# The values product of a 16-head attention with V as the stationary operand in 32-column strips

## The reference

```python
logits = einsum("bhqd,bhkd->bhqk", q, k) / sqrt(16)     # + mask * -1e9, or -inf where masked
attn = softmax(logits, axis=-1)
out = einsum("bhqk,bhkd->bhqd", attn, v)                # back to (b, q, 256), then @ wo + bo
```

## Time and profile before

| | |
|---|---|
| median of 3 runs | 2276.11 us (2273.66 to 2279.21) |
| profiled execution: span from the first to the last instruction | 2271.6 us |
| PE / PEld busy | 1858.7 us (82%) / 1510.4 us (66%) |
| DVE / ACT / POOL busy | 1292.4 us (57%) / 1100.7 us (48%) / 1022.0 us (45%) |
| the chain that ended last | PE 53%, DVE 12%, ACT 7%, issue 5% |
| mean granted clock of TensorE | 0.908 of full speed |

### The profile page before, as it was taken

How to read it: one execution, slowest core, us unless ns; L and a number is a source line. 1 busy time by engine, 2 the same in 40 slices (tenths; PEclk the granted TensorE clock), 3 DMA queues, 4 the chain that set the end, 5 groups by cost and what they waited for, 6 DMA issues and landing times.

```text
span 2271.6 us, 32211 instructions
## 1 busy us (share of the span) xinstructions
PE 1858.7 (82%) x10033; PEld 1510.4 (66%) x10049; DVE 1292.4 (57%) x2343; ACT 1100.7 (48%) x3186; POOL 1022.0 (45%) x911
## 2 busy tenths in 40 slices
PE   4666667566875776776999899999988999999997
PEld 3565556454664664665777777777766787787776
DVE  6877778557558557558445455454533635436361
ACT  1111221446546556556646465564644665556562
POOL 4566665545446436446333354433533423333330
PEclk8889998777887888888999999999989999999999
DMA  7100000000200000000000200000000000000000
GB/s 216 69 5 5 9 5 5 5 1 5 79 1 5 5 1 5 5 0 5 6 1 6 79 0 9 0 5 5 1 5 5 6 6 0 5 23 0 9 1 10
DMA packets 31293, 34.87 MB, mean 15 GB/s; under 512 B 3196, under 2 KB 30040, under 8 KB 30808
## 3 DMA queue, kind: packets, MB, share of 16 engines
q1 hardware_dynamic: 31192, 33.70, 4.7%
HBM read 31.60 MB, written 2.10 MB: 15 GB/s over the span
## 4 chain that ended last, share of the span: by engine, by line
PE 53%; DVE 12%; ACT 7%; issue 5%; POOL 1%; DVEq 0%; ACTq 0%; POOLq 0%
PE ps L496 28%; PE ps L653 9%; PE ps L675 8%; PE ps L663 5%; ACT work L797 4%; DVE xn L843 3%; PE ps L507 3%; DVE shifts L978 1%; ACT hT L718 1%; DVE work L996 1%; ACT work L788 1%; DVE QKb L818 1%; DVE QT L816 1%; DVE work L972 1%; DVE shifts L981 1%
## 5 line engine op out<-in xcount | busy, mean ns | idle before, releaser
L496 PE MATMUL ps<-hT,w_slot 128*128 128x256 f32 x1856 | 449.9, 396 | 27.6 <-ACT hT L718 20.8
L496 PEld LDWEIGHTS ps<-hT,w_slot 128*128 128x128 f32 x1856 | 356.6, 197 | 78.2 <-ACT hT L718 23.7
L1145 POOL TENSOR_TENSOR work<-KT,own_head 128x512 f32<-128x512 f32 x256 | 261.3, 1047 | 289.4 <-ACT KT L730 236.1
L663 PEld LDWEIGHTS ps<-ident,work 128*128 128x128 f32 x1536 | 212.7, 154 | 140.8 <-issue 100.0
L653 PE MATMUL ps<-work,QT 128*128 128x512 f32 x512 | 274.2, 617 | 22.8 <-POOL work L1145 20.6
L855 DVE TENSOR_TENSOR x_all<-ps,x_all 128x512 f32 (+1 forms) x88 | 60.8, 691 | 380.4 <-PE ps L496 331.3
L800 ACT ACTIVATE work<-work,shifts 128x128 f32<-128x128 f32 x768 | 244.8, 392 | 66.4 <-DVE shifts L976 64.8
L663 PE MATMUL ps<-ident,work 128*128 128x128 f32 x1536 | 259.9, 297 | 16.9 <-DVE work L996 16.9
L788 ACT ACTIVATE work<-ps 128x512 f32<-128x512 f32 (+1 forms) x384 | 229.2, 597 | 82.0 <-PE ps L675 54.9
L797 ACT ACTIVATE work<-ps,shifts,score_scale 128x128 f32<-128x128 f32 x512 | 228.3, 471 | 67.7 <-DVE shifts L981 67.7
L675 PEld LDWEIGHTS ps<-V,work 128*128 128x128 f32 x2048 | 251.2, 192 | 7.4 <-issue 4.4
(11 more groups left out here) (114 smaller groups left out, 3040.3 us busy)
## 6 DMA issues: line engine op xcount, KB each, us to landing
ctx_in<-in_ctx SPq DMA_DIRECT2D x32, 256.0 KB, 2.7
w_slot<-in_L_xattn_W SPq DMA_DIRECT2D x2, 1024.0 KB, 6.3
w_slot<-in_L_xattn_ff_w SPq DMA_DIRECT2D x1, 2048.0 KB, 11.3
w_slot<-in_L_xattn_ffn_w SPq DMA_DIRECT2D x2, 1024.0 KB, 8.5
w_slot<-in_L_xattn_w SPq DMA_DIRECT2D x2, 1024.0 KB, 9.8
out<-x_all SPq DMA_DIRECT2D x8, 256.0 KB, 2.1
x_all<-in_x SPq DMA_DIRECT2D x1, 1536.0 KB, 11.6
pad<-in_mask_Bx1x1xS_fk SPq DMA_DIRECT2D x1, 1024.0 KB, 7.2
```

Source lines behind the costliest of these rows:

```text
L496: mm = pe.matmul(dst, lhsT(k), rhs(k), start=(k == 0), stop=(k == chunks - 1))
L663: mm = pe.transpose(bank(2 + u % 2)[:, tok(h)], prob[u % NP][:, tok(h)], ident[:, :])
L1145: pool.tensor_tensor((KBb if quant else KB)[u % NK].rearrange("p (h k) -> p h k", h=HU), keys, own[:, half * HU:(half + 1) * HU].unsqueeze ...
```

## The change

V becomes the stationary operand and the transposed probabilities stream. The output partitions that a strip writes must start at a multiple of 32 and a head is 16 wide, so two heads share a strip: `Vz` holds for each pair four blocks of 16 columns, `[V of head 0, zeros, zeros, V of head 1]`. The product of head `e` takes blocks `2e` and `2e+1` (32 columns), and the two heads of a pair accumulate into the same 32 output partitions. A unit of 4 heads is still 4 products, alternating between two strips. The output has its 256 features on the partitions, so in layers 1 to 3 `outputs` writes `OT`, and the transposes of `O` and their copy go.

The column of ones goes too. In layers 2 and 3 VectorE reduces the exponentials (`row_sums`, two units late), and per sequence takes the reciprocals and spreads them over 16 columns a head (`inverses`). TensorE turns these with two transposes (`inverse_rows`), ScalarE copies them out (`inv_T`), and VectorE multiplies (`outputs`, a step later than before). `O` of the two streams serves as the buffers for the inverses. The vector columns are loaded into `gate`, the quantised V lies in `Vz`'s space, and only four query biases are kept scaled. `Vz` is zeroed once by GpSimd and once more by VectorE before layer 2.

```diff
-        V = two("V", [P, G, H, DH + 1])
+        Vz = two("Vz", [P, G, H // 2, 4, DH])
...
+        Vzb = [b.rearrange("p g a x d -> p (g a x d)")[:, 0:G * D].bitcast(BF16).rearrange("p (g a x d) -> p g a x d", g=G, x=4, d=DH) for b in Vz]
...
+        oinv = rowinv
+        inv_cols = O[0].rearrange("p g (h d) -> p g h d", h=H)
+        inv_T = O[1].rearrange("p g (c t) -> p g c t", c=C)
...
+                sp.dma_start(gate[c0:c0 + n, 0, 0:P], src_of(name).rearrange("(c p) -> c p", p=P)).then_inc(s["vrows_loaded"], 16)
...
+        SUMS_AT = 2
...
-                        pe.wait_ge(s["o_ready"], G * (phase("mix", layer, g, n["mix"] - 1, st) + 1))
-                        turned(one, O[st]).then_inc(q["ot_ps"], 1)
+                        if layer == 0:
+                            pe.wait_ge(s["o_ready"], G * (phase("mix", layer, g, n["mix"] - 1, st) + 1))
+                            turned(one, O[st]).then_inc(q["ot_ps"], 1)
                     elif piece == "y":
-                        pe.wait_ge(q["ot_ready"], use("out", layer, g, n["out"]) + 1)
+                        if layer == 0:
+                            pe.wait_ge(q["ot_ready"], use("out", layer, g, n["out"]) + 1)
+                        else:
+                            pe.wait_ge(s["o_ready"], G * (phase("mix", layer, g, n["mix"] - 1, st) + 1))
                         for j in range(G):
                             mm = product(other[:, j * D:(j + 1) * D], lambda k: OT[st][:, k, tok(j)], lambda k: w[arg["w"]][:, k, :], C)
                         mm.then_inc(q["y_ps"], 1)
...
                 def values(u):
-                    j = u // UJ
+                    j, m = u // UJ, u % UJ // 2
                     pe.wait_ge(s["PT_ready"], U * ap + u + 1)
                     if u % UJ == 0:
                         pe.wait_ge(s["o_ready"], G * (mp - 1) + j + 1)
-                    for h in range(HU):
-                        hh = u % UJ * HU + h
-                        rhs = Vb[st][:, j, hh * DH:(hh + 1) * DH] if quant else V[st][:, j, hh, :]
-                        mm = pe.matmul(bank(4 + j)[:, hh * width:(hh + 1) * width], (PTb if quant else PT)[u % 2][:, tok(h)], rhs,
-                                       start=True, stop=True)
+                    for e in range(2):
+                        for x in range(2):
+                            pair = u % UJ * 2 + x
+                            at = pair % 4 * 32
+                            lhsT = (Vzb if quant else Vz)[st][:, j, pair, 2 * e:2 * e + 2, :]
+                            mm = pe.matmul(bank(4 + j)[at:at + 32, m * S:(m + 1) * S], lhsT, (PTb if quant else PT)[u % 2][:, tok(2 * x + e)],
+                                           start=(e == 0), stop=(e == 1))
                     mm.then_inc(s["o_ps"], 1)
+                def inverse_rows(j):
+                    pe.wait_ge(s["inv_cols_ready"], G * np_ + j + 1)
+                    for m in range(C):
+                        mm = pe.transpose(bank(4 + j)[:, D + m * S:D + (m + 1) * S], inv_cols[:, j, m * HC:(m + 1) * HC, :], ident[:, :])
+                    mm.then_inc(s["inv_ps"], 1)
                 def step(i):
                     if i < U:
                         scores(i)
                     if 0 <= i - lag < U:
                         turn(i - lag)
-                    if 0 <= i - lag - 1 < U:
-                        values(i - lag - 1)
+                    u = i - lag - 1
+                    if 0 <= u < U:
+                        values(u)
+                        if not quant and u % UJ == UJ - 1:
+                            inverse_rows(u // UJ)
...
-                    elif piece == "ot":
+                    elif piece == "ot" and layer == 0:
...
+                    u = i - lag - 1
+                    if not quant and 0 <= u < U and u % UJ == UJ - 1:
+                        j = u // UJ
+                        act.wait_ge(s["inv_ps"], G * np_ + j + 1)
+                        act.activation(inv_T[:, j, :, :].rearrange("p c t -> p (c t)"), bank(4 + j)[:, D:2 * D], ACT.Copy)\
+                            .then_inc(s["inv_T_ready"], 1)
...
-                            quantise(Vb[st].rearrange("p g d -> p (g d)"), O[st].rearrange("p g d -> p (g d)"), other, d, at, q["v_ready"], G)
+                            quantise(Vzb[st].rearrange("p g a x d -> p (g a) x d")[:, :, 0:4:3, :],
+                                     O[st].rearrange("p g d -> p (g d)"), other, d, at, q["v_ready"], G)
...
+                            if j == 0 and layer == 2 and n["att"] == 0 and isinstance(g, int) and g == 0:
+                                dve.memset(Vz[st][:, :, :, :, :], 0.0).then_inc(s["V_zeroed"], 1)
+                                dve.wait_ge(s["V_zeroed"], st + 1)
+                            dve.tensor_tensor(Vz[st][:, j, :, 0:4:3, :], other[:, j * D:(j + 1) * D].rearrange("p (a x d) -> p a x d", x=2, d=DH),
+                                              row(arg["b"] % "v").rearrange("p (a x d) -> p a x d", x=2, d=DH), ALU.add).then_inc(q["v_ready"], 1)
...
+                def row_sums(u):
+                    dve.wait_ge(s["exp_ready"], U * ap + u + 1)
+                    dve.tensor_reduce(rowsums[:, u * HU:(u + 1) * HU], prob[u % NP].rearrange("p (h k) -> p h k", h=HU), AX.X, ALU.add)\
+                        .then_inc(s["sums_ready"], 1)
+                def inverses(j):
+                    dve.wait_ge(s["sums_ready"], U * np_ + UJ * (j + 1))
+                    dve.reciprocal(oinv[:, j, :], rowsums[:, j * H:(j + 1) * H]).then_inc(s["oinv_ready"], 1)
+                    dve.wait_ge(s["oinv_ready"], G * np_ + j + 1)
+                    dve.wait_ge(s["inv_ps"], G * (np_ - 1) + j + 1)
+                    inv = oinv[:, j, :].unsqueeze(2).broadcast_to([P, H, DH])
+                    if masked and arg["mask"] == "drop":
+                        dve.tensor_scalar(inv_cols[:, j, :, :], inv, live[:, 2:3], None, ALU.mult).then_inc(s["inv_cols_ready"], 1)
+                    else:
+                        dve.tensor_copy(inv_cols[:, j, :, :], inv).then_inc(s["inv_cols_ready"], 1)
                 def outputs(j):
                     dve.wait_ge(s["o_ps"], U * ap + UJ * (j + 1))
+                    o = bank(4 + j)[:, 0:D].rearrange("p (c t) -> p c t", c=C)
                     if quant:
-                        dve.tensor_scalar(O[st][:, j, :], bank(4 + j)[:, 0:D], out_scale[:, arg["quant"]:arg["quant"] + 1], None, ALU.mult)\
+                        dve.tensor_scalar(OT[st][:, :, tok(j)], o, out_scale[:, arg["quant"]:arg["quant"] + 1], None, ALU.mult)\
                             .then_inc(s["o_ready"], 1)
                         return
-                    o = bank(4 + j)[:, 0:H * (DH + 1)].rearrange("p (h d) -> p h d", h=H)
-                    nth = G * use("att_phase", layer, g, ST * mix + st) + (j + 1 - G * BEFORE["att_phase"][2])
-                    dve.reciprocal(oinv[:, j, :].unsqueeze(2), o[:, :, DH:DH + 1]).then_inc(s["oinv_ready"], 1)
-                    dve.wait_ge(s["oinv_ready"], nth)
-                    inv = oinv[:, j, :].unsqueeze(2).broadcast_to([P, H, DH])
-                    if masked and arg["mask"] == "drop":
-                        dve.scalar_tensor_tensor(out=O[st][:, j, :].rearrange("p (h d) -> p h d", h=H), in0=o[:, :, 0:DH],
-                                                 scalar=live[:, 2:3], in1=inv, op0=ALU.mult, op1=ALU.mult).then_inc(s["o_ready"], 1)
-                    else:
-                        dve.tensor_tensor(O[st][:, j, :].rearrange("p (h d) -> p h d", h=H), o[:, :, 0:DH], inv, ALU.mult)\
-                            .then_inc(s["o_ready"], 1)
+                    dve.wait_ge(s["inv_T_ready"], G * np_ + j + 1)
+                    dve.tensor_tensor(OT[st][:, :, tok(j)], o, inv_T[:, j, :, :], ALU.mult).then_inc(s["o_ready"], 1)
...
+                    u = i - SUMS_AT
+                    if not quant and 0 <= u < U:
+                        row_sums(u)
+                        if u % UJ == UJ - 1:
+                            inverses(u // UJ)
+                    u = i - lag - (1 if quant else 2)
...
+            for n, name in enumerate(Q_BIASES):
+                at = col_at[name][0]
+                q_bias = dve.tensor_scalar(vcols_q[:, n * C:(n + 1) * C], bank(0)[:, at:at + C], float(DH) ** -0.5, None, ALU.mult)
+            q_bias.then_inc(s["tables_ready"], 1)
...
-                pool.memset(V[st][:, :, :, :], 1.0).then_inc(s["consts_ready"], 1)
+                pool.memset(Vz[st][:, :, :, :, :], 0.0).then_inc(s["consts_ready"], 1)
...
```

More of the change, by code:

```diff
@@ L102 @@
 PER_PASS["local_phase"] = [ST * n for n in PER_PASS["local"]]
+PER_PASS["natt_phase"] = [ST * (a - q) for a, q in zip(PER_PASS["att"], PER_PASS["qatt"])]
 PER_PASS["masked_phase"] = [ST * sum("mask" in arg for _, arg in layer) for layer in STEPS]
-FROM_ONE = ("post", "yadd", "tin", "ffn",  "mix_phase", "att_phase", "local_phase")
+FROM_ONE = ("post", "yadd", "tin", "ffn",  "mix_phase", "att_phase", "natt_phase", "local_phase")
```

(15 more changed lines are left out.)

17 lines of the change are left out of this document (5 added, 12 removed).

## The result

The changed kernel takes 2294.45 us (median of 4 runs, 2293.24 to 2294.68), and the kernel before 2274.89 in runs on the same chips. The ratio is 1.0085, with a 95% interval of 1.0071 to 1.0099: slower by 0.85%, where 2297 us was predicted. The spans of the two profiled executions differ by the same amount, 2291.5 - 2271.6 = 19.9 us. The number came out right by luck: as the rest shows, it was the sum of two wrong terms whose errors nearly cancel.

What follows compares the result with a forecast made beforehand. TensorE, 94.4% busy, was taken to bound layers 2 and 3; in layer 1 nothing ruled alone. Terms +17 + 10 - 13 + 6 + 1 = +21 us on 2276 gave 2297 us, range 2215 to 2385.

Steps and rivals of the forecast that it cites:

- Faster: Whole kernel: the time falls because changes of shape cost little or nothing; chance 0.39.
- slower: Whole kernel: the time rises, all cases other than faster or netting to nothing; chance 0.53.
- Values product, layers 2 and 3, +17 us: TensorE's 256 values blocks: 0.55 us overlapped strips plus 0.32 us borders, 0.87 against 0.80 us a unit, +17 us.
- Rival A with half the tails: Borders of the values blocks: shape changes cost 0.16 us a unit, layer 1 half, giving 2253 us; chance 0.21.
- Row sums on VectorE, +6 us: VectorE, layers 2 and 3: row sums delay LayerNorm pieces, 19 waits on xn x 0.3 us; bounds 0 and +45.
- rival C: VectorE's queue becomes the wait: row sums delay xn and the shift, +45 us, 2308 us in all; chance 0.05.
- Layer 1, +10 and -13 us: Layer 1: shape changes around 128 values units, +10 us; output transposes and their copy leave the chain, -13 us.
- ScalarE, inverses and small edits: Layers 2 and 3: ScalarE's busy time +11 us, hidden; inverse turn costed at nothing; small edits +1 us.
- A in full: Borders of the values blocks: shape changes cost nothing, 0.25 us a unit saved, -66 us, 2210 us; chance 0.18.
- B: Values blocks: strips don't overlap, 1.2 us a unit with borders, +105 us in all, 2381 us; chance 0.15.

Runs made afterwards that it cites:

- e6: Changed kernel with the values product's two loops exchanged and both pairs of heads on one strip, half the output overwritten: 2354.77 us, ratio 1.0344.
- e8: Changed kernel with the values product's loops exchanged and one extra full-width transpose between each block's two strips: 2450.79 us, ratio 1.0754.
- e5: Changed kernel with the values product's two loops exchanged, four instructions on one strip, then four on the other: 2297.28 us, ratio 1.0099.
- e4: Kernel before the change, with the 256 row-sum reduces added on VectorE and nobody reading them: 2321.15 us, ratio 1.0197.
- e3: Changed kernel with row sums accumulated by ScalarE in its exponentials and no reduce on VectorE: 2263.09 us, ratio 0.9946.
- e1: Changed kernel with each row sum on VectorE replaced by a short instruction that writes ones: 2262.79 us, ratio 0.9946.

## Why the prediction was right, and where it wasn't

*Time and sign*: 2297 predicted, 2294.45 measured, +21 against +19.6 us. Faster had 0.39 and slower 0.53. By its own steps:

*Values product, layers 2 and 3, +17 us*: wrong in sign. The step that failed is the block's size, 0.55 us of overlapped slots and 0.32 us of borders. It measured 0.65 in all: 0.43 for the fullest strip (e6) and 0.22 for two borders (e8 gives 0.13 for one, the changed kernel's timeline 0.09 in front and 0.13 behind). So -0.15 us a unit where +0.07 stood, and -35 us of TensorE's busy time. The strips counted 5 slots of 8 because only neighbours in the order were taken to overlap; it is 4, the fullest strip's, in any order (e5). So 0.43 us lies below the lower bound of 0.55, while the borders lie within theirs (0 to 0.62). Rival A with half the tails (0.71 us a unit) was the nearer description of TensorE. By the drain that the Trainium skill (TensorEngine Tiling, Key Properties) states, the borders should cost something, and the trace agrees: the loads stop for 0.17 and 0.20 us.

*Row sums on VectorE, +6 us*: the right mechanism, mis-sized by a factor of five to eight. TensorE idled 55 us more in layers 2 and 3, 46 of them on xn; e4 measures 45 us for the load alone, and taking it off VectorE gives 32 (e3). The upper bound (+45, two row sums in one chain) was about the true value, and the chain in front of xn has just these two. But it got there by another sum: of e4's 45 us 31 are waiting and 16 are TensorE's lower clock, which no term had. I had priced 19 places at 0.3 us. There were 31 in e4 and 35 in the changed kernel; that TensorE was close to waiting in many more places than 19 is the likely reason, and no run shows it. That VectorE was only 46% busy said nothing on this: what counts is what stands in front of the one instruction that TensorE waits for. It was counted as rival C, with 0.05.

*Layer 1, +10 and -13 us*: the net of -3 was near. It starts its first values product at 437.2 us in both kernels and gives over to layer 2 0.5 us earlier (1115.6 against 1116.1), with a zeroing of 0.91 us in between. The two terms were not measured apart. The mean granted clock there is 0.82, against 0.81.

*ScalarE, inverses and small edits*: no cost was expected of the inverse turn; TensorE waits 5.8 us for it, and its 128 transposes are busy 28.0 us where those of O were 21.7. ScalarE's busy time moved by 3 us.

*The luck*: the values product came out 52 us below its term, and idle time rose 55 us where 6 were forecast. These two errors cancel to 3 us. TensorE's -35 us isn't fully accounted for either: 38 us off the blocks, with a lower clock (11 us by e1) and the inverse turn against it, leave some 10 us without a cause that a run shows.

*Rivals*: A and C were both true and stood as alternatives, while each alone was off by more than the forecast. A in full would have needed free borders. B is excluded by e6, which makes it true: 0.99 us a block and 2354.8 us (B said 2381), and the changed kernel lies 60 us below it.

The forecast could have been made better from the rows it had. The wait on xn was already TensorE's longest, and the row sum was put into exactly the queue that ends in it, twice per LayerNorm. 32 mixes x 1.4 us was worked out and set aside.

## What to carry to other kernels

An engine at 46% can still be the wrong place for new work when its fixed order has a short chain in it for which the bounding engine waits: count the instructions that come to stand in front of that wait, and put them behind it (18 us here) or on an engine with room (32 us). Products with 32-column weights pay when several strips are filled between two changes of shape, since a block costs its fullest strip plus two borders. And a predicted total that comes out right proves none of its terms; adding one suspect to the old kernel (e4) is a cheap way to price it.

## What the runs showed of the hardware

- f32 products with 32-column weights on different strips stream together, at 0.107 us an instruction of 128 columns on each: 8 on one strip 0.99 us to the next full-width product, 8 on two strips 0.56 to 0.57, 16 on four strips 0.57. The order in which the two strips are issued made no difference (e5, 0.57 us): a matmul of the second strip starts beside the first strip's although three more of the first strip's stand in front of it. I had not expected that.
- A change between full-width and strip products costs about 0.09 to 0.13 us at a granted clock of 1.00 (e8, and the changed kernel's timeline). In the weight loads it shows as a stop of 0.17 to 0.20 us.
- Accumulating row sums in ScalarE's exponentials adds a read of 192 to 246 ns a head, but only some 80 us of ScalarE's busy time for 1024 of them (e3).
- Waiting costs TensorE clock as well. After 2.30 us of idling its granted clock was 0.50 for the next 2.6 us, and four transposes took 1.09 us instead of 0.48. Over layers 2 and 3, e4's TensorE was busy 16 us longer for the matmuls of the kernel before.
